# A decoder layer on one core: weights folded in four quarters from a host layout, homes for all 32 experts, and a step's filling and emptying apart

## The reference

```python
# 1. causal attention on layernorm(x), added to x
f = h @ w_kv_a                                  # 256 -> 192 (q latent) + 64 (kv latent) + 64 (k rope)
q = rmsnorm(f_q) @ w_qb                         # 16 heads of 128 + 64 (rope)
k, v = split(rmsnorm(f_kv) @ w_kvb)             # 16 heads of 128 + 128
x += softmax(mask(q @ k.T * 192 ** -0.5)) @ v @ w_o
# 2. a cross step on layernorm(x): two linears whose weights are the inputs fside and ctx of this
#    batch, both quantized to int8 steps, with clip(round(.), -127, 127); silu gate between
# 3. a mixture of experts on layernorm(x): router (32 experts, 8 groups, best 3 groups, best 4 experts),
#    at most 40 tokens kept per expert, gate/up/down of each expert, plus one shared expert
```

## Time and profile before

| | us |
|---|---|
| median of 3 runs | 443.41 |
| lowest, highest | 442.05, 449.01 |
| the profiled execution | 444.59 |
| its span in the trace | 442.8 |
| TensorE busy | 356.5 (81%) |
| DVE, POOL, ACT busy | 249.4, 209.5, 177.0 |

### The profile page before, as it was taken

The page is one execution under the profiler, slowest core; times in us unless marked ns, Lnnn a source line. Parts: engine busy times, 40 slices in busy tenths (PEclk is TensorE's granted clock), DMA queues, the critical chain, the costliest instruction groups (busy, mean ns, idle before and its releaser), DMA issues.

```text
span 442.8 us, 7025 instructions
## 1 busy us (share of the span) xinstructions
PE 356.5 (81%) x2206; PEld 250.0 (56%) x2206; DVE 249.4 (56%) x839; ACT 177.0 (40%) x564; POOL 209.5 (47%) x276
## 2 busy tenths in 40 slices
PE   3299989989999998899898895777677652996980
PEld 2154657656677665675665664565565542553870
DVE  2146464575437686877867976662967660336233
ACT  2123447666616865335774236551132000342000
POOL 3102256676718565359976367742134042000674
PEclk9789999999999999999999999899889685998996
DMA  5999508802000000000000000621000004175353
GB/s 158 206 196 283 169 17 227 242 17 71 1 1 1 0 2 1 0 8 28 7 5 3 1 0 7 179 72 38 0 4 2 19 1 125 48 234 177 89 149 114
DMA packets 45512, 32.14 MB, mean 73 GB/s; under 512 B 8697, under 2 KB 44436, under 8 KB 45348
## 3 DMA queue, kind: packets, MB, share of 16 engines
q1 hardware_dynamic: 42980, 28.45, 24.7%
q0 software_dynamic: 2496, 3.25, 2.9%
HBM read 26.56 MB, written 8.84 MB: 80 GB/s over the span
## 4 chain that ended last, share of the span: by engine, by line
PE 39%; DVE 20%; POOL 10%; issue 10%; ACT 8%; DMA 8%; SPq 4%; POOLq 0%; ACTq 0%; DVEq 0%
PE psum L589 29%; PE psum L598 10%; DMA region_b<-in_L_attn_w_o_dram 3%; POOL expert_rows L1685 3%; DMA region_b<-expert_out,slot_gather 2%; POOL region_b L1699 2%; DVE neg_max L1280 2%; POOL region_t L1653 2%; ACT region_r L974 2%; ACT region_t L1035 1%; POOL rstd L1640 1%; DVE smooth L1341 1%; ACT region_t L974 1%; POOL region_t L1652 1%; SPq L496 1%
## 5 line engine op out<-in xcount | busy, mean ns | idle before, releaser
L589 PE MATMUL psum<-region_h,region_b 128*128 128x256 f32 (+1 forms) x352 | 77.5, 354 | 1.7 <-DVE region_b L1592 1.7
L1652 POOL TENSOR_SCALAR region_t<-region_t,prob_rsums 128x128 f32<-128x128 f32 x64 | 40.9, 639 | 52.2 <-DVE prob_rsums L1274 51.7
L1653 POOL TENSOR_SCALAR region_t<-region_t,prob_rsums 128x256 f32<-128x256 f32 x64 | 64.9, 1013 | 0.0
L1033 ACT ACTIVATE region_t<-psum,neg_max 128x128 f32<-128x128 f32 x64 | 23.8, 372 | 94.5 <-DVE neg_max L1280 94.3
L589 PE MATMUL psum<-region_c,region_h 128*128 128x512 f32 x128 | 61.1, 601 | 0.0
L589 PEld LDWEIGHTS psum<-region_h,region_b 128*128 128x128 f32 x352 | 52.4, 193 | 5.9 <-DVE region_b L1592 2.1
L1699 POOL DMA_INDIRECT region_b<-expert_out,slot_gather x20 | 20.7, 1036 | 48.1 <-DMA expert_out<-region_h 42.3
L1685 POOL DMA_INDIRECT expert_rows<-h_moe,slot_scatter x32 | 33.3, 1042 | 18.4 <-DVE slot_scatter L1528 11.4
L598 PE MATMUL psum<-consts,region_t 128*128 128x128 f32 x192 | 32.0, 275 | 10.6 <-ACT region_t L974 9.9
L598 PEld LDWEIGHTS psum<-consts,region_t 128*128 128x128 f32 x192 | 22.3, 141 | 31.8 <-issue 18.4
L1279 DVE TENSOR_REDUCE neg_max<-psum 128x1 f32<-128x128 f32 x64 | 18.1, 282 | 38.8 <-PE psum L589 38.4
(11 more groups left out here) (204 smaller groups left out, 693.1 us busy)
## 6 DMA issues: line engine op xcount, KB each, us to landing
region_a<-in_L_ffn_W_gate_dram SPq DMA_DIRECT2D x17, 128.0 KB, 2.5
region_a<-in_L_ffn_W_up_dram SPq DMA_DIRECT2D x17, 128.0 KB, 2.6
region_a<-in_L_ffn_W_down_dram SPq DMA_DIRECT2D x17, 128.0 KB, 2.7
region_b<-in_L_attn_w_o_dram SPq DMA_DIRECT2D x2, 1024.0 KB, 13.8
expert_out<-region_h SPq DMA_DIRECT2D x8, 256.0 KB, 3.1
expert_rows<-region_g SPq DMA_DIRECT2D x10, 132.5 KB, 4.2
region_b<-in_L_ffn_W_gate_dram SPq DMA_DIRECT2D x10, 128.0 KB, 2.5
region_b<-in_L_ffn_W_up_dram SPq DMA_DIRECT2D x10, 128.0 KB, 2.5
```

What stands on the lines that cost most here:

```text
L589: return nc.tensor.matmul(out_, lhsT, rhs, start=first, stop=last)
L1033: nc.scalar.activation(probs[:, hn % 4, 0:P], s[:, 0:P], ACT.Exp, bias=nmax[:, hn, 0:1], accum_out=sums[:, hn, 0:1])
L1652: g.tensor_scalar(pr[:, 0:P], pr[:, 0:P], rsum[:, hn, 0:1], None, ALU.mult)
L1653: g.tensor_scalar(pr[:, P:3 * P], pr[:, P:3 * P], rsum[:, hn, 1:2], None, ALU.mult).then_inc(sg["probs_normed"], 1)
```

## The change

**Host layout.** The weights reach the device in the layout that SBUF wants: `fold_w` is four quarters (four heads each) with rows of 9 KB per partition, already transposed where `prepT` did it; `rope_w` likewise, with the K=64 part held twice, on partitions 0 to 63 and 64 to 127; fside and ctx transposed; router and shared weights transposed in one tensor; each expert one tensor of 3 KB rows. Gammas and bias ride with the constants. `prepT`, `rwT`, `shT` and TensorE's and ACT's part of `wx` are gone.

**Start.** Attention begins when quarter 0 is folded (`prepM` 0 and 1) and one pair of q units is ready; `prepM` 2 to 7 and the second chunk move into the first heads. `prepM` takes two banks, and ACT copies its `w_mo`.

**q.** A step covers both tiles of a batch. The K=64 products of the two tiles use the two halves of the rows, with no zero padding. There are four buffers for q instead of two.

**Filling and emptying apart.** A step such as `probsT` has a second entry `*probsT` later in the list. TensorE works by the first, all others by the second. Inside a head the order is `SLOT`. `probsT` and `q` take banks of the ring, which now has five.

**Experts.** All 32 have a home, in regions that come free earlier; one load each, none of them waits for an expert group.

**Small.** The mask is one product over 256 columns, the key halves are swapped in `kT` to allow it; the two clamps ahead of rounding go.

```diff
-BANK_S, BANK_PT, BANK_O, BANK_Q, BANK_W = 0, 2, 3, 4, 5
+BANK_S, BANK_O, BANK_W = 0, 2, 3
...
-EVEN_SLOT = ("scores", 0, "norm", 1, "q", "probsT", 2, "qT", 3)
-ODD_SLOT = ("norm", "scores", "rope", 0, "probsT", 1, "pv", 2, 3)
+SLOT = ("scores", "exp", "*pv", "*q", 0, "rope", "probsT", "max", "norm", 1, "*probsT", "qT", "pv", 2, "q", 3, "*qT")
+SPLIT = ("q", "qT", "probsT", "pv", "hT", "fused", "latT", "prepM", "x_T", "x_back", "x_qT", "x_mm",
+         "x_back2", "x_qT2", "x_mm2", "r_T", "r_logit")
...
-PREP_AT = (5, 12)
-FRONT_AT, FRONT_GAPS, FRONT_NEXT = (6, 36, 50), (0, 2, 5, 8), 4
+PREP_AT = (0, 1, 5, 7, 12, 16)
+FRONT_AT, FRONT_GAPS, FRONT_NEXT = (20, 40, 54), (0, 2, 5, 8), 4
...
+    def place(at, step):
+        places[at].append(step)
+        if step[0] in SPLIT:
+            places[at + 1].append(("*" + step[0],) + step[1:])
...
-             ("prepT", 0), ("latents", 0), ("prepT", 1), ("latents", 1), ("latT", 0), ("prepM", 0),
-             ("prepT", 2), ("latT", 1), ("prepT", 3), ("prepM", 1), ("prepT", 4), ("prepT", 5), ("q", 0, 0),
...
+             ("latents", 0), ("prepM", 0), ("latents", 1), ("latT", 0), ("prepM", 1), ("latT", 1), ("q", 0, 0),
+             ("rope", 0, 0), ("rope", 1, 0), ("qT", 0, 0), ("qT", 1, 0)]
+    for p, at in zip(range(2, 8), PREP_AT):
+        place(at, ("prepM", p))
+    place(3, ("q", 0, 1))
...
+def tensor_steps(steps):
+    return [step for step in steps if step[0][0] != "*"]
+
+def other_steps(steps):
+    later = {step for step in steps if step[0][0] == "*"}
+    kept = [step for step in steps if ("*" + step[0],) + step[1:] not in later]
+    return [(step[0].lstrip("*"),) + step[1:] for step in kept]
...
+            for c in range(NQ):
+                sp.dma_start(fold[c].rearrange("p h m -> p (h m)"), fold_w[c]).then_inc(ld_fold[c], 16)
+                sp.dma_start(wf[:, c, :, HC * KL:], rope_w[c].rearrange("p (k n) -> p k n", k=2)
+                             ).then_inc(ld_rope_cols[c], 16)
+                if c == 1:
+                    load_x(1)
...
-            for e in range(NHOME, E):
-                if (e - NHOME) % XG == 0:
-                    wait_filled(sp, ("dn", (e - NHOME) // XG))
-                load_expert(e)
...
-                    mm(bank(step), qn0[:, t, :], wf0[:, HC * c:HC * (c + 1), :], True, False)
-                    fills(mm(bank(step), qn1[:, t, :], wf1[:, HC * c:HC * (c + 1), :], False, True), step)
+                    for j, item in enumerate(pair):
+                        wait_emptied(pe, ("latT", NJ * b + j))
+                        wait_empty(pe, item)
+                        mm(bank(item), qn0[:, NJ * b + j, :], wf[:, c, 0, :], True, False)
+
+                    for j, item in enumerate(pair):
+                        half = slice(j * KL, (j + 1) * KL)
+                        fills(mm(bank(item), qn1[half, b, :], wf[half, c, 1, :], False, True), item)
...
-                    mm(o[:, 0:P], id_bf[:], mask_bf[:], True, False)
-                    mm(o[:, 0:P], q[:, 0:P], kT[:, b, 0:P], False, True)
-                    mm(o[:, P:3 * P], q[:, P:2 * P], kT[:, b, :], True, False)
-                    mm(o[:, 2 * P:3 * P], id_bf[:], mask_bf[:], False, True).then_inc(sg["scores_ready"], 1)
+                    mm(o[:, 0:2 * P], id_bf[:], mask_bf[:], True, True)
+                    nc.tensor.matmul(o[:, 0:P], q[:, 0:P], kT[:, b, P:2 * P], start=False, stop=True,
+                                     skip_group_check=True)
...
-                    for i in range(3):
-                        last = turn(ps_pt[:, i * P:(i + 1) * P], probs[:, hn % 4, i * P:(i + 1) * P])
-                    last.then_inc(sg["probsT_done"], 1)
+                    wait_empty(pe, step)
+                    for i, block_ in enumerate((0, 2, 1)):
+                        last = turn(bank(step)[:, i * P:(i + 1) * P], probs[:, hn % 4, block_ * P:(block_ + 1) * P])
+                    fills(last, step)
...
-                    link(v.tensor_scalar(qa, qa, QMAX, -QMAX, ALU.min, ALU.max))
```

## The result

The changed kernel takes 417.9 us in the median of 4 runs (416.45 to 418.94), the kernel before 442.73 beside it: a ratio of 0.945, interval 0.940 to 0.950. It is faster, and 19 us slower than the 399 forecast. One of the four executions of the kernel before took 449.01 us at a lower granted clock; it is in this median and not in the ratio.

What follows compares the result with a forecast made beforehand. Attention was taken as bound by TensorE. Start 20.3, attention 18.7, clamps 1.1 and experts 4.4 sum to 44.5 us: span 442.8 becomes 398.3, median 399, with 80 in 100 from 387 to 415.

Steps and rivals of the forecast that it cites:

- the start: Stretch up to the first maximum: it starts at 25.4 us instead of 45.7, 20.3 us gone, bounds 14 to 21.
- the coarse window: Load traffic of 357 GB/s seen with a coarse mix, against 141 with small pieces; used to price the first loads.
- TensorE's work in attention: Attention's 64 heads: work falls from 227.9 to 218.3 us, by q 8.9 and transposes 4.0 less, `prepM` 3.3 more.
- The price of not overlapping: Rival, 10 in 100: the row halves of q do not overlap; 13.3 us in attention, 0.9 at the start: 413.
- The rule that a change of tiling mode drains TensorE: Pairs of q: 0.17 us extra each, taken from `pv`; if that is the drain, 15 times 0.17 = 2.6 us.
- TensorE's idle time in attention: Attention: idle time falls from 23.1 to 14 us, bounds 5 to 32; with the work, 18.7 us less.
- 9.9 for the bank: Attention: 9.9 us of waits for ACT's copy from the one probabilities bank go, as `probsT` walks five banks.
- 10.7 for POOL: Attention: 10.7 us of TensorE's waits for POOL's normalising stay or grow.
- The rival of the in-order queues: Attention, 14 in 100: in-order queues become the bound, POOL cannot catch up; idle 23 to 32 us, 408 to 417.
- The rival of the start alone: 4 in 100: the gain is only the start; attention stays at 245 to 250 us, 412 to 418.
- the experts: Experts' stage: no 2.50 us load wait, no lower clock behind it; 4.4 us less, bounds 2.5 and 5.
- The clamps: Two clamps ahead of rounding in the last batch's chain go: 1.1 us; the six others count nothing.

Runs made afterwards that it cites:

- The fixed bank: The changed kernel with all transposes of probabilities (`probsT`) going to one fixed bank again and a ring of four: 418.75 us, 0.945 against the kernel before.
- four gaps altered: The changed kernel, cross step of batches 0 and 1: transpose one place earlier, smoothing factor, way back and product one later each: 410.07 us, 0.928.
- all seven: The changed kernel, cross step of batches 0 and 1: `x_T` one place earlier, six later gaps one place wider each: 410.94 us, 0.925.

## Why the prediction was wrong

**Right: the start.** 18.8 for 20.3 us. The first quarter had landed before 12.09 us, where its products begin without a wait; the coarse window of the earlier trace rows was the right one to price it by (287 to 402 GB/s in the slices of the start now). The chain behind it took 1.5 us more than summed. What the forecast counted as moved work was moved, as the run with all folding first shows.

**Right: TensorE's work in attention.** Forecast 218.3, measured 215.6 us. The step that carried it is the pair of `q`, 2.88 for 2.83 us. The price of not overlapping, 13.3 + 0.9, came out as 13.5 us of time in part by luck: the work grew by 21.1, and a third of that was taken up by idle time. The rule that a change of tiling mode drains TensorE (the Trainium skill, TensorEngine Tiling, Key Properties) was read from 0.17 us. The pair here has 0.23 us more than three times 0.885, which is of that size, but the trace does not single a drain out: records of full rows follow each other in 0.43 us, and the two records of one half-row product, with no change of mode between them, in 0.53.

**Wrong: TensorE's idle time in attention.** The step was 14 us for 23.1; it was 29.4. This is nearly the whole miss: 15.4 us, where the spans differ by 16.4 (414.7 and 398.3); start, experts and the steps between added 4, TensorE's work took 3 off. Two things failed in it. First, the two waits of the earlier trace rows were taken as two amounts: 9.9 for the bank, which goes, and 10.7 for POOL, which stays. They are on two lists, the first of TensorE's products and the second of its weight loads. TensorE's own list before sums to about 23 us without the second, and nine of its eleven stops for the bank are stops of the weight load for POOL as well. One of them:

```profile
210.07 1.38 POOL L1653 TENSOR_SCALAR region_t<-region_t,prob_rsums 128x256 f32<-128x256 f32 x1
...
211.21 0.53 ACT L974 ACTIVATE region_t<-psum 128x384 f32<-128x384 f32 x1
...
211.86 0.31 PEld L598 LDWEIGHTS psum<-consts,region_t 128*128 128x128 f32 x3 [2.37 <-POOL region_t L1653]
211.89 0.52 PE L598 MATMUL psum<-consts,region_t 128*128 128x128 f32 x3 [2.06 <-ACT region_t L974]
```

POOL's scaling ends at 211.45, ACT's copy at 211.74. With the bank free this stop would still have lasted until POOL was through: 0.3 of its 2.06 us were to be had from the bank. The same reading of all eleven stops gives some 4 us instead of 9.9, an estimate from their rows. Second, the forecast took a wait to vanish with the resource that it names. The fixed bank shows that it does not: with the bank gone or back, idle time is 29.4 or 29.7 us. POOL's normalising, which the forecast kept at 10 us or more, went as well, to 0.7, and idle time rose all the same. What is taken away at one step is met at the next; the run with the row halves apart shows the exchange from the other side, with 21.1 us more work and 6.1 us less idle time. Which result sets the 29.4 us is shown for single gaps only and stays open.

The rival of the in-order queues had this mechanism and its price (idle 23 to 32, 408 to 417), and got 14 in 100, because POOL's mean load of three quarters spoke against it. A mean load says little here: POOL is at 32 to 43 us of some 60 per batch (before it was 34 to 45; the prediction's 37 to 45 leaves out the second batch), and still late at the one instruction that counts. The rival of the start alone, 412 to 418 with 4 in 100, holds the measured time too, but 6 us came from attention. By the windows, all that the change brings up to the last maximum is TensorE's work: 27.7 + 227.9 = 255.6 us before, 13.4 + 215.6 = 229.0 now, 26.6 less; its idle time is 40.4 and 42.0.

**Half right: the experts.** TensorE's part went as forecast, with no wait for a load. But of the 4.4 us 2.1 arrived. The chain of waits shows the last store of the results, from issue to landing, after and before:

```profile
378.91 3.95 DMA expert_out<-region_h
```

```profile
408.48 2.14 DMA expert_out<-region_h
```

1.8 us were given back there; up to the start of this store the stage is 4.0 us shorter. The prediction had the stores keep their length. The view of the DMA queues for the time of the store in the changed kernel has one packet that is not the store's:

```profile
q8 instruction: 1, 0.02, 2.2%
```

It is a load of 16 KB of instructions, from 380.03 to 381.39 us. All packets of the store are through by 380.7 but 16 of 1 KB, a sixteenth of its data, as one of the 16 DMA engines would have it; these run from 381.38 on, and the store lands at 382.86. In the kernel before, the packet comes at 410.48, when the store's data is through. The same holds in all twenty traces: the sixteen whose last store takes 3.7 to 4.5 us have such a packet in the middle of it, the four with 2.14 to 2.16 us have not. No run moved the packet on purpose. The run in which the last experts wait for their loads again loses nothing, so that the late homes as such carried none of the gain.

**The clamps.** The stretch up to the experts became 0.8 us shorter for the 1.1 forecast.

**The range** ended 3 us short. The stated bounds of the idle term reach to 32 us, 18 above the value taken, and so to 417; the range stopped at 415, on a chance of 14 in 100 for the case that came true.

**What beats both.** The changed kernel with four gaps altered takes 410.1 us (0.928), with all seven 410.9 (0.925).

## What to carry to other kernels

Count the work that a change takes off the bound engine, and expect that; a wait of that engine in a fixed order is not a sum to be collected, for it is charged again to the next late result. Before summing waits, see that they come from one list, and look in the timeline at what else ends just before the one that is named. When an order is written by hand, a change of it should be followed by a search over its gaps, since moving one kind of step cost 13 to 17 us in three kernels here, and altered gaps gained 3 to 8 us in six runs, nothing in two, and cost 10 us in the kernel before.

## What the runs showed of the hardware

- Two f32 products on the two halves of the rows, 512 columns each, run side by side when they follow each other: a pair of units takes 2.88 us, and 4.11 with a full product between the halves. The page TensorE: Matmul & The Clock Gate of the Trainium skill (What overlaps and what doesn't) has matmuls start and end in order; the trace agrees, the records of the two halves start at 56.59 and 56.60 us, and that order does not keep the second half from running during the first.
- The granted clock of a stage moves with small edits, and the work with it: the same products took 215.3 us of work at 0.98, 223.6 at 0.94 (with 7.5 us more idle time) and 213.0 at 0.99 (with 4 us less). The idle time alone does not tell the grant: it was 26.1 us at 0.96 and 29.4 at 0.98.
- The last store of 256 KB took 3.7 to 4.5 us in the sixteen traces in which a 16 KB load of instructions fell into it, and 2.14 to 2.16 in the four in which none did. In the changed kernel the last sixteenth of its data ran alone, right behind that load.
